# 16-bit window offsets for TensorE's register loads, and the row tables of three edge groups made by GpSimd

## What is computed

```
def _L0_gnn_ref(x, nnz_weight, bias, edge_index):
    row, col = (edge_index[0], edge_index[1])
    W = jnp.zeros((OUTDIM, INDIM), dtype=nnz_weight.dtype).at[row, col].add(nnz_weight)
    return x @ W.T + bias

def _sage_layer(h, edge_src, edge_dst, deg_inv, W_self, W_neigh, b):
    msg = h[edge_src]
    agg = jax.ops.segment_sum(msg, edge_dst, num_segments=h.shape[0])
    mean = agg * deg_inv[:, None]
    return h @ W_self + mean @ W_neigh + b

h = jnp.maximum(_layernorm(x, axis=-1), 0.0)
x = x + _L0_gnn_ref(h, edge_weight, L0_gnn_bias, edge_index)
h = jnp.maximum(_layernorm(x, axis=-1), 0.0)
x = x + _L1_gnn_ref(h, src, dst, ...)      # two sage layers, relu between them
```

## Time and profile before

| | |
|---|---|
| median of 3 runs | 769.54 us (769.11 to 769.72) |
| the profiled execution | 768.53 us |
| its span, first to last instruction | 766.5 us |
| TensorE busy | 747.6 us, 98% |
| VectorE busy | 572.1 us, 75% |
| ScalarE busy | 353.5 us, 46% |
| GpSimd busy | 473.6 us, 62% |

### The profile page before, as it was taken

How to read it: one execution, slowest core, us unless ns; L and a number is a source line. 1 busy time by engine, 2 the same in 40 slices (tenths; PEclk the granted TensorE clock), 3 DMA queues, 4 the chain that set the end, 5 groups by cost and what they waited for, 6 DMA issues and landing times.

```text
span 766.5 us, 13521 instructions
## 1 busy us (share of the span) xinstructions
PE 747.6 (98%) x4453; PEld 620.8 (81%) x4454; DVE 572.1 (75%) x819; ACT 353.5 (46%) x593; POOL 473.6 (62%) x593
## 2 busy tenths in 40 slices
PE   3999999999999999999999999999999999999998
PEld 2878888888888888888788888888888888887887
DVE  7999677877465797986779685446598857569885
ACT  7977623433353452366336745542223323245731
POOL 3000366667579999865656373436999875645992
PEclk9999999999999999999999999999999999999999
DMA  3123467665586854567683536776743868785475
GB/s 117 50 74 111 115 217 257 204 227 179 167 289 198 295 157 133 172 218 253 211 271 116 165 120 197 253 247 208 272 142 104 254 199 286 234 288 185 144 235 202
DMA packets 82984, 148.78 MB, mean 194 GB/s; under 512 B 10809, under 2 KB 21108, under 8 KB 82912
## 3 DMA queue, kind: packets, MB, share of 16 engines
q1 hardware_dynamic: 62974, 105.18, 44.0%
q10 hardware_dynamic: 19938, 42.69, 15.8%
HBM read 106.42 MB, written 41.41 MB: 193 GB/s over the span
## 4 chain that ended last, share of the span: by engine, by line
PE 97%; DVE 2%; issue 1%; DMA 0%; DVEq 0%
PE bank L1765 50%; PE bank L1819 21%; PE bank L1690 14%; PE bank L1575 4%; PE bank L1563 1%; PE bank L1596 1%; PE bank L1837 1%; PE bank L1586 1%; PE bank L1681 1%; PE bank L1592 1%; DMA dst_g<-in_dst 0%; DVE L L2004 0%; DVE R L1989 0%; PE bank L1604 0%; DVE low L1883 0%
## 5 line engine op out<-in xcount | busy, mean ns | idle before, releaser
L1765 PE MATMUL bank<-slot,split 128*128 128x512 f32 x1128 | 261.7, 390 | 0.5 <-issue 0.5
L1765 PEld LDWEIGHTS bank<-slot,split 128*128 128x128 f32 x1128 | 210.9, 188 | 44.2 <-issue 0.9
L1085 POOL TENSOR_TENSOR AT<-AT,az 128x50 int32 (+3 forms) x288 | 94.6, 329 | 115.8 <-DMA az<-asum_scratch 72.9
L1765 PE MATMUL bank<-slot,split_third 128*128 128x512 f32 x552 | 129.7, 390 | 0.0
L1765 PEld LDWEIGHTS bank<-slot,split_third 128*128 128x128 f32 x552 | 103.1, 188 | 21.4 <-issue 0.2
L1819 PE MATMUL bank<-slot,Ax 128*128 128x512 f32 (+1 forms) x510 | 119.1, 388 | 0.3
L1819 PEld LDWEIGHTS bank<-slot,Ax 128*128 128x128 f32 x510 | 93.4, 188 | 20.0 <-issue 1.4
L2149 DVE TENSOR_TENSOR slot<-T,slot 128x512 fp32r<-128x512 f32 x64 | 84.3, 1328 | 25.9 <-ACT slot L1348 22.0
L1690 PE MATMUL bank<-slot,split_m 128*128 128x512 f32 x320 | 87.9, 396 | 0.0
L1141 POOL TENSOR_TENSOR T<-T,wst 128x512 f32<-128x512 f32 x48 | 65.1, 1375 | 4.9 <-DMA wst<-in_L_gnn_W_self 4.9
L1690 PEld LDWEIGHTS bank<-slot,split_m 128*128 128x128 f32 x320 | 58.5, 188 | 11.4 <-issue 0.2
(11 more groups left out here) (234 smaller groups left out, 1196.2 us busy)
## 6 DMA issues: line engine op xcount, KB each, us to landing
stage<-hT_scratch SPq DMA_DIRECT2D x90, 256.0 KB, 3.8
wst<-in_L_gnn_W_neigh SPq DMA_DIRECT2D x56, 256.0 KB, 4.6
wst<-in_L_gnn_W_self SPq DMA_DIRECT2D x56, 256.0 KB, 3.6
x1b_scratch<-x ACTq DMA_DIRECT2D x10, 512.0 KB, 5.6
hT_scratch<-hTs ACTq DMA_DIRECT2D x10, 512.0 KB, 3.1
wst<-prod0g_scratch SPq DMA_DIRECT2D x20, 256.0 KB, 3.5
hT_scratch<-h1s ACTq DMA_DIRECT2D x20, 256.0 KB, 3.3
wst<-prod1g_scratch SPq DMA_DIRECT2D x20, 256.0 KB, 3.4
```

Source lines behind the costliest of these rows:

```text
L1085: pool.tensor_tensor(a, a, az32[:, n % NZ, pairs * pos:pairs * (pos + 1)], ALU.add) \
L1765: last = pe.matmul(dense_bank(v, which)[:, :], split_tile(v, a)[:, NT * k:NT * (k + 1)], slot[t % 2][:, b, HF * (HK * which + k):HF * (HK ...
```

## The change

Two edits. The offsets for TensorE are kept in 16 bits: a table `tab_go` of 40 x 8 uint16 is written by VectorE in place of the columns of `tab_g`, and `tab_o` is uint16. And the rows of groups 18, 26 and 34 are compared by GpSimd, eight instructions a group, each of one chunk (125 x 128, with the src value of each edge as a scalar of its partition), into a buffer `rows_p` of three groups beside the ring R. VectorE leaves these three comparisons out. TensorE counts `s_made` accordingly, waits for a further semaphore in these groups, and takes its weights from `rows_p`. GpSimd's instructions stand behind its last mask.

```diff
+ROWS_BY_POOL = (18, 26, 34)
...
-        tab_o = sb("tab_o", [1, NG * GC], I32, build)
+        tab_o = sb("tab_o", [1, NG * GC], U16, build)
...
+        tab_go = sb("tab_go", [NG, GC], U16, build)
...
+        rows_p = sb("rows_p", [EP, len(ROWS_BY_POOL), GC, P], BF16, build)
...
+        def made_by(j):
+            return 2 * (j + 1) - sum(p <= j for p in ROWS_BY_POOL)
+
+        def row_of(j, c):
+            if j in ROWS_BY_POOL:
+                return rows_p[:, ROWS_BY_POOL.index(j), c, :]
+            return R[:, j % NR, c, :]
...
             sp.wait_ge(s_tab, 1)
-            sp.dma_start(tab_o[:, :], tab_g[:, OFFW:OFFW + GC]).then_inc(s_tabo, 16)
+            sp.dma_start(tab_o[:, :], tab_go[:, :]).then_inc(s_tabo, 16)
...
+            pool.wait_ge(s_key, 1)
+            for n, j in enumerate(ROWS_BY_POOL):
+                for c in range(GC):
+                    last = pool.tensor_scalar(rows_p[:, n, c, :], iota[:, :], slo[:, j, c:c + 1], None, ALU.is_equal)
+                last.then_inc(s_pooled, 1)
...
-                    last = pe.matmul(a_bank(n)[:, at:at + ka(j)], R[:, r, c, :], L[:, q, c, 0:ka(j)],
+                    last = pe.matmul(a_bank(n)[:, at:at + ka(j)], row_of(j, c), L[:, q, c, 0:ka(j)],
...
-                    row = R[:, r, c, :]
+                    row = row_of(j, c)
...
-                pe.wait_ge(s_made, 2 * j + 2)
+                pe.wait_ge(s_made, made_by(j))
+                if j in ROWS_BY_POOL:
+                    pe.wait_ge(s_pooled, ROWS_BY_POOL.index(j) + 1)
...
-            dve.tensor_scalar(tab_g[:, OFFW:OFFW + GC], shift[:, :], float(TW), None, ALU.mult).then_inc(s_tab, 1)
+            dve.tensor_scalar(tab_go[:, :], shift[:, :], float(TW), None, ALU.mult).then_inc(s_tab, 1)
...
-                if j > 0:
+                if j > 0 and j not in ROWS_BY_POOL:
                     hot_rows(R[:, j % NR, :, :], slo2[:, j, :, :]).then_inc(s_made, 1)
```

More of the change, by code:

```diff
@@ L475, in build_program @@
         s_made = sem("s_made")
+        s_pooled = sem("s_pooled")
         s_hot = sem("s_hot")
@@ L1556, in sums_of_A @@
             def sums_of_A(j):
-                q, r = j % NQ, j % NR
+                q = j % NQ
                 for c in range(GC):
```

## The result

The changed kernel takes 817.26 us (median of 5 runs, 816.32 to 817.73), the kernel before 769.11 us (767.93 to 769.72) on the same chip: a ratio of 1.0622 (95% interval 1.0607 to 1.0636), 48 us more. The forecast was 768.7, with a range up to 772.0. The profiled execution took 817.69 us, its span is 816.0.

A forecast was written before the change was run, and what follows sets the result against it. TensorE was bound by its own order, VectorE close behind. VectorE at group 36 decided: 75.15 - 1.8 + 2.5 + 0.15 = 76.0 against 76.83, 0.8 us earlier; 769.54 - 0.8 = 768.7 us, range 766.7 to 772.0.

The forecast's parts named there:

- the price of edit 1's load: TensorE's load of eight 16-bit offsets: 0.306 us instead of 0.59, gaining 0.285; the other bound was no gain.
- rival 4: The 16-bit load goes one value at a time, 2.4 us instead of 0.59, some 56 us slower; chance 0.06.
- Its count of 31 groups: Groups in which the one-by-one load would cost TensorE 1.8 us more each, some 56 us in all.
- The price by register: Rival count for TensorE's offsets load: about 200 ns per register, 1.6 us for eight, no gain; set aside; no separate chance.
- In groups 2 to 5 the load counts in full: There the load stands ahead of the A sums, so all its gain reaches TensorE: 4 x 0.285 = 1.1 us.
- VectorE's distance as a cap: At group 36 VectorE is 1.68 us ahead of TensorE; less 0.15, edit 1 alone could gain 1.53 us.
- A turn costs VectorE 0.10 us: Each GpSimd comparison alternating with VectorE in groups 2 to 10 costs VectorE 0.105 us, 24 turns, 2.5 us.
- 2.5 against 1.8, so 0.7: Edit 2 on VectorE: 24 turns cost 2.5 us, three groups' rows left out spare 1.8 us.
- turns from 13 us on with all done near 28: GpSimd's 24 comparisons start about 13.2 us, alternate with VectorE and end with group 10, before group 18 needs them.
- 1.5 us of TensorE at group 8: VectorE, slowed by 20 turns, is ready at 25.65 instead of 23.40, so TensorE takes group 8 up 1.5 us later.
- Rival 3: In groups 2 to 10 VectorE's two-table instructions wait out GpSimd's whole instruction: 3.5 us slower, 773.0; chance 0.12.
- 0.4 us in hand for a later rise: Building stage: TensorE's clock rising a group later costs 0.21 us on one zeroing matmul, about as much on others.

The follow-up runs named there:

- runs 3 to 7: Offsets' load in turn: 16-bit cut in two (820.6 us), 32-bit cut in two (797.1), 32-bit low halves (817.1), every second 32-bit word (819.1), 16-bit as words (777.97).
- run 10: Kernel before, with TensorE loading only four of a group's eight 32-bit offsets and using each for two chunks: 767.57 us, ratio 0.9981.
- runs 2 and 12: Run 2, and its kernel with group 12's rows made behind the weighing, so that VectorE pauses once: the latter 769.09 us, ratio 0.9997.
- run 11: Run 10 plus GpSimd comparing the rows of groups 18, 26 and 34: 767.40 us, ratio 0.9983 to the kernel before.
- run 2: Changed kernel with the offsets table in 32 bits again, leaving only GpSimd's rows: 770.16 us, ratio 1.0013 to the kernel before.
- run 7: Changed kernel's 16-bit table, rows all on VectorE, eight offsets read as four 32-bit words and taken apart in TensorE's sequencer: 777.97 us, ratio 1.0125.
- run 1: Kernel before with only the offsets table in 16 bits, rows all on VectorE: 818.16 us, ratio 1.0644.

## Why the prediction was wrong

**The step that failed** is the price of edit 1's load: "eight values of 2 bytes go like the shortest load, 0.306". It measured 1.92. The prediction bounded the term by "nothing is gained" and by the shortest load, so a loss was outside its bounds; it stood in rival 4 alone, 8 x 0.304 = 2.4 us, at 0.06, with "Nothing in the trace speaks for it". Rival 4 is what happened. Its price was too high, 1.8 more instead of 1.33, because a further value costs 0.233 us and not a whole single load. Its count of 31 groups left out groups 2 to 5, where the load stands ahead of the A sums. 35 x 1.33 = 46.6.

**Why it was taken.** The earlier trace rows have loads of one, eight and nine values. 16 bytes a step and one value in 0.30 fit them, as the prediction said, and so does what runs 3 to 7 show: four neighbouring words that begin at a multiple of 16 bytes at once, all else one by one. The rows had no load of two or three values. A load of two would have read 0.54 us, more than half of eight, and would have shown that values are read singly unless something special holds.

**The price by register.** The Trainium skill's page "Runtime: NRT & Kernel Launch" (Instruction fetch mechanics) has about 200 ns for each register, even in bulk. The page speaks of loads from HBM, these come from SBUF. The prediction put the figure aside, since eight took 0.59. The trace is near it for everything but aligned neighbours: 233 ns for each further register in the changed kernel, 1.92 for eight against the 1.6 that the prediction had worked out from it. So counting by register was the right rule for the new load; the row that was taken to refute it was of the one kind of load that is an exception.

**What held.**
- TensorE bound from end to end, the building stage's loss reaching the end unchanged: 48.8 us there, 49.5 in the span.
- In groups 2 to 5 the load counts in full: run 10 is 1.03 us earlier by group 5 (without the later start), 4 x 0.257. At group 6 it waits 0.5 us for VectorE.
- VectorE's distance as a cap: 1.53 forecast, 1.4 us measured (run 10), there with fewer register operations as well.
- A turn costs VectorE 0.10 us: rows 0.771 against 0.672, keys 0.49 against 0.39 (runs 2 and 12).
- Edit 2 costs VectorE more than it spares, 2.5 against 1.8, so 0.7: 0.5 by the trace of run 11 against run 10.

**What was wrong in edit 2.** Not in turns from 13 us on with all done near 28, but standing still until 38 us and the last begun at 66 us; not 1.5 us of TensorE at group 8, but none there and 1.1 at group 18 (run 2). GpSimd's comparison takes 0.60 us alone, where the select's 0.28 had been taken. That all 24 are done with group 10, and the waits of TensorE cost nothing, is the step that fails; in the changed kernel the slow loads hide it. Rival 3, full blocking, had the wrong engine held: GpSimd pays, and not VectorE. The Trainium skill's page "SBUF — State Buffer" (Who interferes with whom) has the later one block fully. Up to 38 us the trace agrees in that one side is held and the other not (17.5 us of one comparison, VectorE's rows at 0.672), though the comparison stood through 47 instructions of VectorE; from 38 us on VectorE loses only 0.10 us a turn.

**The pace of the W sums.** The prediction had TensorE bound by the order of A sums, old W, zeroing, load and W sums. It read nothing of the register operations between the W sums, though from group 12 to 25 they, and not the matmuls, set the W sums' pace: 0.93 us a group with eight of them, 0.69 with four (run 10), and 1.34 in run 7, where the load is as short as in run 10 and the registers are taken apart as well. A TensorE that was busy 9.45 to 10 of 10 us was paced by its sequencer. The 1.77 us a group that the prediction worked out from the count of matmuls is 1.84 from start to start (groups 20 to 36, 47.44 to 76.83); nothing hung on it.

**The sum.** With a load of 0.33 us the forecast for both edits was 0.8 us faster; run 11 is 1.3 faster (0.5 to 2.2). That is no confirmation: the halved register operations let TensorE catch up behind group 18, and its wait there, 5.3 us, was not in the sum. How much the changed kernel would have gained with a short load and all else as it is stays open.

**The clock.** The prediction had 0.4 us in hand for a later rise. What came was 4.5 us of slower matmuls in the changed kernel, which fits the idling as its cause and not the other way round: run 1 has the same loss with ten long zeroing matmuls, not twelve.

None of the runs is a version that computes all of the reference and beats the kernel before. The 1.4 us of runs 10 and 11 come with four words and four register operations a group instead of eight, and VectorE caps more.

## What to carry to other kernels

Before a table of register values is narrowed or laid out anew, count its reads and not its bytes: keep it in 32 bits, as neighbours that begin at a multiple of 16 bytes, and load them in fours. Count the register operations between the matmuls too. A run that is to price one of them must keep the others as they were, which runs 10 and 11 here did not. Where a price is extrapolated to a type that the trace does not have, its bounds must reach beyond "no gain" to the cost of handling every value alone. And work given to an idle GpSimd beside a VectorE that never pauses is not done when its own durations say; put the deadline behind VectorE's next pause.

## What the runs showed of the hardware that was not expected

- A load of registers from SBUF: 0.30 us for one value and 0.233 for each further. Four neighbouring 32-bit words from a multiple of 16 bytes count as one, 0.33, so two words (0.54) cost more than four, and eight 0.59. 16-bit values, words with gaps and words off that boundary go singly.
- A register operation of TensorE's sequencer ahead of each chunk's three W sums stands 0.115 us behind the last one, and so paces matmuls that could go faster: 24 in 0.93 us with eight operations, in 0.69 with four.
- Taking packed registers apart is not free: 0.13 us of TensorE's sequencer for two values.
- GpSimd's one-input comparison stood for 17.5 us beside a VectorE without a pause, nearly all of whose instructions had two tables as input, at no cost to VectorE. After a gap of 0.03 us it ended within 0.44 us, and turns followed in some cases, at 0.10 us each for VectorE.
